# Second cross attention: all ten key blocks of the softmax denominators added by TensorE, the POOL sums removed

## The reference, cut to what matters

```
scores = jnp.einsum('bgnqd,bgkd->bgnqk', qg, k) * scale
scores = jnp.where(causal, scores, -1e30)
attn = jax.nn.softmax(scores, axis=-1)           # exp(s - max) / sum over the keys
out = jnp.einsum('bgnqk,bgkd->bgnqd', attn, v)
x = x + tanh(g_xattn[1]) * (out @ w_out.T)
```

## Time and profile before

| what | value |
|---|---|
| time, median of 3 runs (lowest to highest) | 837.15 us (835.89 to 839.64) |
| the profiled execution: its own time, its span | 839.7 us, 837.9 us |
| busy: PE matmul, PE weight load, DVE, ACT, POOL | 662.7, 362.7, 644.6, 610.9, 383.5 us |
| the 16 sums of `summed` on POOL | 55.9 us busy, 3495 ns each |
| `xattn1`, from the first `scores` to the end of `attended(15)` | about 340 to 669 us of the span |

### The profile page before, as it was taken

One profiled execution on the slowest core, in us unless ns is written; L12 is line 12 of the kernel. 1 busy time (PEld: TensorE's weight loads), 2 busy tenths in 40 slices (PEclk: granted clock), 3 DMA queues, 4 the chain that ended last, 5 costly groups with the idle time before them and its releaser, 6 DMA issues. The chain is left out here.

```text
span 837.9 us, 13670 instructions
## 1 busy us (share of the span) xinstructions
PE 662.7 (79%) x5174; PEld 362.7 (43%) x5174; DVE 644.6 (77%) x978; ACT 610.9 (73%) x814; POOL 383.5 (46%) x493
## 2 busy tenths in 40 slices
PE   8853367876767756679989896989999799888886
PEld 6421123332333323445654564555646444444443
DVE  3689999999999896895885489556635448888884
ACT  3787699989968993488884587658937427767775
POOL 1016526656684775273373148311303416565652
PEclk9996589999979988779999999899999889999999
DMA  8900300000000000622331021112300000100011
GB/s 309 388 2 0 133 18 2 1 0 1 1 0 2 1 0 1 226 70 70 81 120 35 1 70 37 48 40 69 114 1 2 5 31 1 39 26 26 26 38 50
DMA packets 21906, 43.72 MB, mean 52 GB/s; under 512 B 3921, under 2 KB 8529, under 8 KB 21073
## 3 DMA queue, kind: packets, MB, share of 16 engines
q1 hardware_dynamic: 21840, 42.85, 15.0%
HBM read 38.61 MB, written 4.19 MB: 51 GB/s over the span
## 5 line engine op out<-in xcount | busy, mean ns | idle before, releaser
L1660 DVE TENSOR_REDUCE c_nmax<-c_s 128x1 f32<-128x384 f32 (+3 forms) x176 | 108.7, 634 | 83.7 <-PE c_s L1878 83.7
L1778 ACT ACTIVATE c_probs<-c_e 128x512 f32<-128x512 f32 (+1 forms) x176 | 94.6, 559 | 57.7 <-PE c_e L1908 56.7
L1590 POOL TENSOR_TENSOR c_psum<-c_probs 128x1536 f32<-128x1536 f32 x16 | 55.9, 3495 | 156.4 <-ACT c_probs L1778 156.4
L1362 PE MATMUL b_y<-w2q,b_q2T 128*128 128x512 bf16 x256 | 71.8, 433 | 54.5 <-ACT b_q2T L1279 30.1
L2227 PE MATMUL d_gu<-gateq,d_xqT 128*128 128x512 bf16 (+1 forms) x384 | 84.0, 362 | 14.1 <-ACT d_xqT L2152 13.8
L1875 PE MATMUL c_s<-c_kT,c_qaT 96*128 96x128 f16 (+3 forms) x256 | 73.1, 319 | 22.8 <-DVE c_nmax L1660 20.5
L1333 PE MATMUL b_up<-shared,b_xqT 128*128 128x512 bf16 x256 | 70.9, 402 | 2.7 <-ACT hidden L1245 2.7
L1906 PE MATMUL c_e<-c_qaT,c_kT 98*128 98x512 f16 (+3 forms) x256 | 69.8, 307 | 3.4 <-ACT c_qaT L1765 2.8
L1362 PEld LDWEIGHTS b_y<-w2q,b_q2T 128*128 128x128 bf16 x256 | 25.8, 107 | 91.4 <-issue 43.7
L2227 PEld LDWEIGHTS d_gu<-gateq,d_xqT 128*128 128x128 bf16 x384 | 35.1, 98 | 50.4 <-ACT d_xqT L2152 19.8
L1875 PEld LDWEIGHTS c_s<-c_kT,c_qaT 96*128 96x128 f16 x256 | 25.6, 101 | 68.0 <-DVE c_nmax L1660 39.5
(11 more groups left out here) (245 smaller groups left out, 1872.2 us busy)
## 6 DMA issues: line engine op xcount, KB each, us to landing
c_stage<-in_gateT SPq DMA_DIRECT2D x16, 704.0 KB, 4.0
c_stage<-in_downT SPq DMA_DIRECT2D x6, 768.0 KB, 4.5
xs<-in_x SPq DMA_DIRECT2D x4, 1024.0 KB, 14.9
a_w1f<-in_w1T SPq DMA_DIRECT2D x2, 2048.0 KB, 16.7
hidden<-in_w2T SPq DMA_DIRECT2D x2, 2048.0 KB, 22.3
out<-xs SPq DMA_DIRECT2D x16, 256.0 KB, 2.0
b_ln_g<-in_ln_g SPq DMA_DIRECT2D x1, 1024.0 KB, 4.8
b_ln_b<-in_ln_b SPq DMA_DIRECT2D x1, 1024.0 KB, 8.5
```

The source lines that it names most:

```text
L1362: last = nc.tensor.matmul(y_ps[:], q2T[:, n % 2, c, :], w2q[:, c, :], start=(c == 0), stop=(c == IC - 1))
L1590: nc.gpsimd.tensor_tensor(psum[:], region(slot, 0)[:, :, P:], region(slot, 1), ALU.add).then_inc(psum_ready, 1)
L1660: nc.vector.tensor_reduce(nmax[:, G % 2, i, n:n + heads], s_ps[u % 2][:, 0:heads * (i + 1) * P].rearrange("p (n k) -> p n k", n=heads), ax ...
L1778: nc.scalar.activation(probs[:, G % 2, at:at + width], e_ps[fill % 3][:, 0:width], ACT.Exp).then_inc(e_read, 1)
```

## The change

`summed` and its buffer `psum` are removed, and with them the semaphore `psum_ready`. `total` adds all ten blocks of `probs` directly: 40 matmuls a group instead of 28, in the trace 80 instructions instead of 56. POOL's `inputs.setup`, which writes into a buffer that POOL also uses to turn the queries, gets a wait of its own on the last turned query, `q_ready`.

```
-    psum = t("psum", [P, GROUP, WIDTH[1]])
...
-            def summed(G):
-                slot = G % 2
-                pool.wait_ge(e_read, exp_of(G, 7))
-                if G:
-                    pool.wait_ge(den_done, G)
-                nc.gpsimd.tensor_tensor(psum[:], region(slot, 0)[:, :, P:], region(slot, 1), ALU.add).then_inc(psum_ready, 1)
...
-                G, r = group(u - LAG - 7)
-                if r == 0 and 0 <= G < GROUPS:
-                    summed(G)
                 if u == INPUTS_AT:
                     pool.wait_ge(w_scale_ready, 2)
+                    pool.wait_ge(q_ready, BATCH * TILES)
                     inputs.setup(pool)
...
             def total(G):
                 take("tr", rden_ready, G + 1)
-                pe.wait_ge(psum_ready, G + 1)
                 pe.wait_ge(e_read, exp_of(G, PER - 1))
-                parts = [region(G % 2, 0)[:, :, 0:P]] + [psum[:, :, i * P:(i + 1) * P] for i in range(TILES - 1)]
-                parts = [(i, part) for i, part in enumerate(parts)] + [
-                    (i, region(G % 2, k)[:, :, (i - k) * P:(i - k + 1) * P]) for k in (2, 3) for i in range(k, TILES)]
+                parts = [(i, region(G % 2, k)[:, :, (i - k) * P:(i - k + 1) * P]) for k in range(TILES) for i in range(k, TILES)]
                 for m, (i, part) in enumerate(parts):
                     for n in range(GROUP):
                         last = nc.tensor.matmul(den_ps[n * HD:(n + 1) * HD, 0:P], pattern[:, i, :], part[:, n, :],
```

More of the change, by code:

```diff
@@ L1457, in xattn1 @@
     s_done, max_ready, nparts_ready = s("s_done"), s("max_ready"), s("nparts_ready")
-    e_done, e_read, psum_ready = s("e_done"), s("e_read"), s("psum_ready")
+    e_done, e_read = s("e_done"), s("e_read")
     av_done, av_read, den_done, rden_ready, expanded, attn_ready = (
```

## The result

The changed kernel takes 841.0 us (median of 14 runs, 839.65 to 843.51), the kernel before 836.68 us (14 runs, 834.98 to 839.64). The ratio is 1.0051, with a 95% interval from 1.004 to 1.0062, so +4.3 us. A second set of runs gave 841.11 us, again at a ratio of 1.0051.

The account below looks back on a forecast made before the run. PE was taken to set the pace almost everywhere; 9.0 (exposed matmuls) - 0.4 (DVE stalls) - 2.3 (end) - 2.8 (clock) = +3.5 us on a median of 837.15 gave 840.6 us, range 835.8 to 844.8.

Parts of the forecast that it names:

- What bounds the kernel: Second cross attention: PE sets the pace almost everywhere, DVE and ACT have slack, and the wait on `psum_ready` costs nothing.
- The price of 24 instructions, 0.66 us: The 24 instructions added to `total` per group take 0.66 us at full clock, 10.6 us of PE in 16 groups.
- How much is exposed, 9.0 us: Behind the 16 totals: 13 groups count 0.66 us each and total(9) 0.40, together 9.0 us slower.
- two stalls of DVE: At 508.31 and 561.30 us PE waits for a maximum delayed beside POOL's sums; removing them gives 0.4 us back.
- The end, -2.3 us: End of the stage: without the last sum DVE is earlier, the stage ends 2.3 us earlier, total(15)'s added matmuls are hidden.
- The clock, -2.8 us: Hand-over to `ffn1`: PE's 3.08 us gap becomes two of about 1.1, the clock stays up, giving 2.8 us.
- Sum: Whole kernel: 9.0 - 0.4 - 2.3 - 2.8 = +3.5 us, giving 840.6 us.
- The fallen clock: Rival, chance 0.20: the clock falls all the same at the hand-over to `ffn1`; +6.3 us, 843.4.
- Half hidden: Rival, chance 0.13: half of the added matmuls is hidden under DVE's and ACT's own work; -1.0 us, 836.2.
- the freed port: Rival, chance 0.08: DVE carries the stage, so all 9.5 us lost beside POOL's sums come back; -5.6 us, 831.5.
- the dear matmul: Rival, chance 0.03: the 24 added instructions cost 1.2 us a group, the low clock's price; +10.8 us, 848.0.
- The moved wait: POOL's new wait on `q_ready` is met over 100 us ahead of `setup`'s first reader and costs nothing.

Follow-up runs that it names:

- filled kernels: The kernel before and the changed kernel, each with extra unread matmuls in PE's waits; ratios to the kernel before 0.9979 (835.24 us) and 1.0045 (840.22 us).
- last_sum_gone: Kernel before with only group 15's sum on POOL removed and ten blocks added by total there; 0.9963 of the kernel before, 835.04 us.
- thirteen_blocks: Changed kernel with three blocks of key tile 1 added twice, 24 more instructions a group; 1.0196 of the kernel before, 852.08 us.
- three_sums_gone: Kernel before with POOL's sums removed and ten blocks in total only for groups 3, 7 and 15; 0.995 of the kernel before, 833.59 us.
- sums_gone_alone: Changed kernel with total adding only seven blocks, key tile 1 left out, so no added matmuls; 0.9931 of the kernel before, 832.05 us.
- matmuls_alone: Kernel before with total adding all ten blocks while POOL still makes its unread sums; 1.0134 of the kernel before, 848.4 us.

## Why the prediction was right, and where its terms were off

- **What bounds the kernel.** Right. 24 instructions of PE pass through to DVE's and ACT's waits one for one, twice over (1.34, 1.99, 2.65 us).
- **The price of 24 instructions, 0.66 us.** Right: 80 take 2.39 us with the tail of the last, and successive totals move apart by 0.65 to 0.66 us where nothing absorbs it. By the gap of about 56 ns that the Trainium skill ("TensorE: Matmul & The Clock Gate", section "Back-to-back issue gap") gives for an isolated matmul it would have been an estimated 1.34 us, and by the 81 ns that the same section gives for a stream of weight loads and matmuls, which is what the trace has here, an estimated 1.94 us. The trace agrees with neither: at full clock it is 0.66 us.
- **How much is exposed, 9.0 us, less 0.4 for two stalls of DVE.** Mis-sized: 6.9 us net at full clock. Total(3) counted with 0.66 us and is hidden; the cast L383 gives 0.3 back; and the stalls around groups 7 and 9 give 0.4 each instead of 0.2. A stall of DVE was worth more than the wait that PE showed next behind it. That DVE stays late through the following units is my reading; it was not tried by itself.
- **The end, -2.3 us.** Right: 7.95 to 5.78 us, so -2.2, and with the one sum removed alone the same 5.79.
- **The clock, -2.8 us.** The term that failed. It took one execution's low stretch as a fixed cost of the program, and the shorter gap as what would keep the clock up. The filled kernels put what the clock costs in the median at 1.8 us before and 0.5 to 0.9 us after, so the change gets about 1 us from it and not 2.8. The other way round, the filled traces differ by 4.8 us and the medians of the plain kernels by 4.3 (3.3 to 5.2), which leaves 0.5 us for the clock (-0.4 to 1.5). And the gap does not decide: five traces have the same two waits of PE at the hand-over, 1.17 and 1.12 us (the changed kernel twice, last_sum_gone, thirteen_blocks, three_sums_gone), and in two of the five the projection was slow, 4.80 and 5.08 us.
- **Sum.** With the measured terms: +6.9 - 2.2 - 1.0 = +3.7 us, against 4.3 (3.3 to 5.2) measured. The forecast of 3.5 was as near as that because the errors of the two wrong terms, 1.7 us too much and 1.8 us too much gain, cancelled. That is luck.
- **The rivals.** The fallen clock (843.4) did not come as such, but is partly in the median. Half hidden (836.2), the freed port (831.5) and the dear matmul (848.0) are refuted, in this order by the 6.9 of 9.0 us that came through and by thirteen_blocks, by sums_gone_alone, and by the price of 24 instructions.
- **The moved wait.** In the changed kernel POOL's scales wait for DVE's first input, and `setup` ran at 534 us, 130 us ahead of that. It costs nothing, as said.

Left open: the profiled executions of the kernel before were 3.0 and 1.4 us above the medians of their sets, and both had a slow projection. How often the clock falls at the hand-over in the other executions is not known. The mean clock over the whole span is on record for each execution: 0.918 to 0.926 in the kernel before, whose profiled ones have 0.925, and 0.928 to 0.933 in the filled one. That suggests that the clock falls somewhere in every execution of the kernel before, and no less in those that were faster; so the low time alone does not give the cost. In the profiles a low stretch cost 0.2 us at 432 us and 2.8 us at the hand-over; 1.8 us is only what the medians show.

## What to carry to other kernels

Work moved to the engine that sets the pace costs its full issue time, so move it only at the places where that engine waits, and read those places in a profile in which its clock was not low just there: a slow engine hides its own waits. An idle engine's large operations are not free if they hold up a busy one: one sum of 3.5 us at the hand-over cost 2.2 us, the other fifteen together gave back less than their matmuls cost. Where the same operation is cheap in some groups and dear in others, decide for each group; three of sixteen changed here gave 4 us (3.1 of them came with the last one alone), all sixteen lost 4.

## What the runs showed of the hardware that was not expected

- The granted clock of one program differs between executions: the changed kernel had no low stretch between 376 and 690 us in one profile and three in the next, and its stage differed by 2.4 us. Waits of 2.42 and 2.43 us at the same place were followed by a low clock in one and not in the other. A profile's low stretches are no fixed cost.
- PE's idle stretches can be used to hold the clock at its upper level: 49 unread matmuls in five waits kept it at 1.00 from 376 to 690 us and made the kernel before 1.8 us faster (0.9979, 0.997 to 0.9987).
- Which of two instructions is stretched where they meet goes with when they start. A clip of 1536 columns on DVE that started 0.68 us behind a 3.44 us sum on POOL took 3.57 us and ended 0.8 us behind the sum; the same clip 0.05 us behind the same sum kept its 0.90 us, and the sum took 4.25 us instead, in each of the seven traces that have this pair. So a delay elsewhere can create such a stall, as in matmuls_alone.
